# A four-layer graph network on one core: index loads over 96 partitions, counting on two engines, the step table before the first node table, and padding rows of their own

## The reference, cut to what matters

```
h = x @ W                                   # layer 0, attention (self loops included)
alpha = softmax over edges of dst of leaky_relu(h@att_src [src] + h@att_dst [dst])
x = layernorm(x + sum over edges of alpha * h[src] + bias)

f = ssp(edge_attr_128 @ We1 + be1) @ We2 + be2          # layer 1, filtered messages
x = layernorm(x + x + ssp(segment_sum((x @ Wn)[dst] * f, by src) @ W2 + b2) @ W3 + b3)

x = layernorm(x + normalised graph convolution(x @ W.T) + b)       # layer 2
x = layernorm(x + relu((x + segment_sum(x[src])) @ W1 + b1) @ W2 + b2)   # layer 3
```

## Time and profile before

| | us |
|---|---|
| median of 3 runs | 5233.95 (5231.75 to 5244.96) |
| profiled execution | 5240.87 |
| its span | 5239.2 |
| PE busy | 2666.3 (51%) |
| DVE busy | 2713.4 (52%) |
| ACT busy | 1384.4 (26%) |
| POOL busy | 3533.9 (67%) |

### The profile page before, as it was taken

The page is one execution under the profiler, slowest core; times in us unless marked ns, Lnnn a source line. Parts: engine busy times, 40 slices in busy tenths (PEclk is TensorE's granted clock), DMA queues, the critical chain, the costliest instruction groups (busy, mean ns, idle before and its releaser), DMA issues. The chain is left out here.

```text
span 5239.2 us, 54126 instructions
## 1 busy us (share of the span) xinstructions
PE 2666.3 (51%) x13249; PEld 2200.9 (42%) x13329; DVE 2713.4 (52%) x7266; ACT 1384.4 (26%) x4147; POOL 3533.9 (67%) x3833
## 2 busy tenths in 40 slices
PE   1477777777688854344434534344443243434444
PEld 1355656556466643333333433333333233333333
DVE  2599888887788853333333433333333433333333
ACT  4497666666566720000000400000000200000002
POOL 0677777777255567777777377777777477777773
PEclk8799899998677765555555755555555555555556
DMA  3677666677377742122112122222223322222224
GB/s 76 175 172 173 160 162 159 161 173 152 64 228 230 231 123 53 51 53 53 52 51 52 45 56 52 52 52 53 53 53 49 58 53 51 51 51 53 53 53 52
DMA packets 430928, 489.98 MB, mean 94 GB/s; under 512 B 86459, under 2 KB 333071, under 8 KB 430614
## 3 DMA queue, kind: packets, MB, share of 16 engines
q0 software_dynamic: 131904, 288.49, 23.4%
q1 hardware_dynamic: 295828, 197.27, 14.0%
q10 hardware_dynamic: 2882, 0.70, 0.1%
HBM read 359.63 MB, written 126.50 MB: 93 GB/s over the span
## 5 line engine op out<-in xcount | busy, mean ns | idle before, releaser
L1521 PE MATMUL bank<-arena 128*128 128x128 f32 x4992 | 1276.9, 438 | 1952.1 <-DVE arena L893 1639.4
L1595 POOL DMA_INDIRECT arena<-node_table,pick x1664 | 1599.2, 961 | 633.3 <-issue 506.4
L1521 PEld LDWEIGHTS bank<-arena 128*128 128x128 f32 x4992 | 1111.7, 328 | 2117.1 <-DVE arena L893 1799.0
L879 DVE TENSOR_TENSOR acc<-acc,bank 128x128 f32 x2496 | 720.9, 289 | 2075.2 <-PE bank L1521 1785.9
L1595 POOL DMA_INDIRECT arena<-gat_table,pick x832 | 863.8, 1038 | 306.6 <-issue 247.8
L1595 POOL DMA_INDIRECT arena<-message_table,pick x832 | 799.6, 961 | 255.8 <-issue 253.2
L1194 ACT COPY xt<-bank 128x512 f32<-128x512 f32 (+1 forms) x39 | 21.6, 554 | 2128.7 <-PE bank L1465 2128.7
L893 DVE TENSOR_TENSOR arena<-iota_free,local 128x512 f32<-128x512 f32 x624 | 427.9, 686 | 7.2 <-DMA node_table<-x_sb 4.0
L1510 PE MATMUL bank<-arena 128*128 x1664 | 324.9, 356 | 50.8 <-DVE arena L908 45.3
L1510 PEld LDWEIGHTS bank<-arena 128*128 128x128 f32 x1664 | 278.3, 254 | 115.8 <-issue 115.8
L765 DVE SCALAR_TENSOR_TENSOR acc<-acc,arena,bank 128x129 f32 x832 | 287.5, 345 | 52.8 <-issue 24.2
(11 more groups left out here) (218 smaller groups left out, 3383.8 us busy)
## 6 DMA issues: line engine op xcount, KB each, us to landing
message_table<-arena POOLq DMA_DIRECT2D x208, 256.0 KB, 3.5
filter_table<-arena SPq DMA_DIRECT2D x196, 256.0 KB, 3.6
arena<-filter_table SPq DMA_DIRECT2D x624, 64.0 KB, 2.5
xt<-edge_cols SPq DMA_DIRECT2D x131, 256.0 KB
arena<-local_rows SPq DMA_DIRECT2D x208, 128.0 KB
arena<-node_table,pick POOLq DMA_INDIRECT x1664
arena<-edge_cols SPq DMA_DIRECT2D x65, 256.0 KB, 3.1
arena<-gat_table,pick POOLq DMA_INDIRECT x832
```

The lines of the kernel that those rows point to most:

```text
L879: e.tensor_tensor(a, a, bank[6 + t % 2][:, s * P:(s + 1) * P], ALU.add).then_inc(sums, 1)
L1521: ins = e.matmul(bank[6 + n % 2][:, s * P:(s + 1) * P], hot[n % 2][:, s, :], gathered[:, slot(n, s), 0:D], start=True, stop=True)
L1595: e.indirect_dma_start(out=dst, out_offset=None, in_=table, in_offset=bass.IndirectOffsetOnAxis(ap=index, axis=0)).then_inc(done, 16)
```

## The change

- `dst`, `src` and `ahead` are each loaded in three pieces: 96 rows, the 97th, and the short 98th. `dst` is first, then `ahead`, then `src`; `src` counts on the semaphore of `ahead`.
- ACT, and no longer SP, issues the load of `x`, ahead of its counting. ACT counts the first 29 borders of the first list and needs `dst` alone for it; DVE counts the other 20, by a comparison with an accumulated sum, behind its keys and ahead of the weights.
- The making of the layer-0 table moves behind the branch, into the step table: after `start_e` is made (L468), before DVE waits for the blocks and windows. The keys are stored ahead of the table, and the table is stored in five parts.
- The layer-0 table and both node tables get 128 rows more. A padding slot of partition p in `pick[0]` now picks row `NB*P + p`. The rows hold zeros, and `-BIG` as the logit in layer 0. SP writes them into the node tables ahead of its other zeros.

```diff
+ACT_BELOW = 29
+PARTS = {4: (0, 12), 8: (12, 24), 12: (24, 36), 15: (36, 45), len(TRIOS): (45, NB + 1)}
-        gat_table = dram("gat_table", [NB * P, D + 2])
-        node_table = [dram(f"node_table{k}", [NB * P, D]) for k in range(2)]
+        gat_table = dram("gat_table", [(NB + 1) * P, D + 2])
+        node_table = [dram(f"node_table{k}", [(NB + 1) * P, D]) for k in range(2)]
+        count_junk = flip[0:LP, :].bitcast(BF16)[:, 0:SF]
...
             def step_table(i, lo_bits, rows_of_table):
-                        own(e.tensor_scalar(same[:, :], local[0][:, :], P - 0.5, float(NB * P - 1), ALU.is_gt, ALU.mult))
+                        own(e.tensor_scalar(same[:, :], local[0][:, :], P - 0.5, pad_row[:, 0:1], ALU.is_gt, ALU.mult))
...
         def vector(e):
+            own(e.tensor_scalar(pad_row[:, :], iota_part[:, :], float(NB * P), None, ALU.add))
-            e.wait_ge(ahead_loaded, 32)
-            e.wait_ge(index_loaded, 64)
+            e.wait_ge(index_loaded, 48)
+            e.wait_ge(ahead_loaded, 96)
...
             e.tensor_copy(descents[:, :], descents[:, :]).then_inc(keys_made, 1)
+            q = 0
+            for b in range(ACT_BELOW + 1, NB + 1):
+                if q:
+                    after(q)
+                q = own(e.tensor_scalar(count_junk, list_index["dst"][:, :], float(b * P), 0.0, ALU.is_ge, ALU.add,
+                                        accum_out=below[0][:, b:b + 1]))
+            after(q)
+            below_by_v = own(e.tensor_scalar(below[0][:, ACT_BELOW + 1:NB + 1], below[0][:, ACT_BELOW + 1:NB + 1],
+                                             2.0, -float(SF), ALU.mult, ALU.add))
...
-            own(e.memset(acc[:, NB, :], 0.0))
+            own(e.memset(acc[:, NB, 0:D + 1], 0.0))
+            own(e.memset(acc[:, NB, D + 1:D + 2], -BIG))
-            for n in range(len(TRIOS) + 1):
-                ...                                  # L568 to L578, moved
...
             e.wait_ge(list_sorted, 1)
-            run(step_table(0, SRC_BITS, NB * P))
+            table_of_steps = step_table(0, SRC_BITS, NB * P)
+            next(table_of_steps)
+            next(table_of_steps)
+            for n in range(len(TRIOS) + 1):
+                ...                                  # L568 to L578
+            run(table_of_steps)
...
         def scalar(e):
+            e.wait_ge(cleared, 3)
+            e.dma_start(x_sb[:, 0:NB - 1, :], A["x"][0:FULL, :].rearrange("(b p) d -> p b d", p=P)
+                        ).then_inc(x_loaded, 16)
+            e.dma_start(x_sb[0:LAST, NB - 1, :], A["x"][FULL:N, :]).then_inc(x_loaded, 16)
-            run(count_below(0, list_index["dst"]))
+            run(count_below(0, list_index["dst"], ACT_BELOW))
...
         def tensor(e):
             def step_table(i):
-                e.wait_ge(counted, NB * (i + 1))
+                e.wait_ge(counted, ACT_BELOW + NB * i)
+                if i == 0:
+                    e.wait_ge(vec, steps_of_v["below"])
...                                                  # L1335 and L1345 move behind next(table_of_steps)
         def sync(e):
+            MAIN = LP // 16 * 16
+            def row_in(tile, flat, done):
+                e.dma_start(tile[0:MAIN, :], flat[0:MAIN * SF].rearrange("(p f) -> p f", f=SF)).then_inc(done, 16)
+                e.dma_start(tile[MAIN:LP - 1, :], flat[MAIN * SF:(LP - 1) * SF].rearrange("(p f) -> p f", f=SF)
+                            ).then_inc(done, 16)
+                last = flat.shape[0] - (LP - 1) * SF
+                e.dma_start(tile[LP - 1:LP, 0:last], flat[(LP - 1) * SF:].rearrange("(p f) -> p f", p=1)
+                            ).then_inc(done, 16)
+            e.wait_ge(cleared, 1)
+            row_in(list_index["dst"][:, :].bitcast(I32), A["dst"], index_loaded)
             e.wait_ge(cleared, 4)
+            row_in(ahead.bitcast(I32), A["dst"][1:E], ahead_loaded)
+            row_in(list_index["src"][:, :].bitcast(I32), A["src"], ahead_loaded)
...                                                  # weights as before
-            e.wait_ge(table_put, len(TRIOS))
-            e.dma_start(gat_table.rearrange("(b p) d -> p b d", p=P), acc[:, 0:NB, :]).then_inc(gat_table_out, 16)
             e.wait_ge(list_sorted, 1)
             e.dma_start(sorted_keys[0].rearrange("(p f) -> p f", p=P), keys[0][:, :]).then_inc(list_out, 16)
+            for n in PARTS:
+                b0, b1 = PARTS[n]
+                e.wait_ge(table_put, n)
+                e.dma_start(gat_table[b0 * P:b1 * P, :].rearrange("(b p) d -> p b d", p=P), acc[:, b0:b1, :]
+                            ).then_inc(gat_table_out, 16)
             e.wait_ge(gat_ready, 1)
+            for k in range(2):
+                e.dma_start(node_table[k][NB * P:(NB + 1) * P, :], zero_row[:, :]).then_inc(start_in, 16)
```

More of the change, by code:

```diff
@@ L254, in build_program @@
         pad_col = part([P, 1])
+        pad_row = part([P, 1])
         gat_w, att_prod = gathered[:, 4, :], gathered[:, 5, 0:D]
@@ L543, in vector @@
             e.tensor_copy(descents[:, :], descents[:, :]).then_inc(keys_made, 1)
+            q = 0
[7 more added lines that the diff above has]
+                                             2.0, -float(SF), ALU.mult, ALU.add))
+            steps_of_v["below"] = below_by_v
             e.wait_ge(weights_loaded, WEIGHTS_IN)
@@ L1012, in scalar, with count_below @@
             own = Count(sem("scalar_own"))
-            def count_below(i, index):
-                e.wait_ge(index_loaded, 64)
+            def count_below(i, index, last):
+                e.wait_ge(index_loaded, 48)
+                if i:
+                    e.wait_ge(ahead_loaded, 96)
                 e.wait_ge(off_bias_made, 1)
                 e.wait_ge(below_cleared, i + 1)
-                for b in range(1, NB + 1):
-                    if i * NB + b > 1:
-                        e.wait_ge(counted, i * NB + b - 1)
+                for b in range(1, last + 1):
+                    if i * ACT_BELOW + b > 1:
+                        e.wait_ge(counted, i * ACT_BELOW + b - 1)
                     e.activation(sign_junk[:, :], index[:, :], ACT.Sign, bias=off_bias[0:LP, b:b + 1],
@@ L1160, in scalar @@
             e.wait_ge(gat_ready, 1)
-            background = [count_below(1, list_index["src"]), second_list()]
+            background = [count_below(1, list_index["src"], NB), second_list()]
             for t in range(TICKS + 13):
@@ L1328, in tensor @@
                      ).then_inc(descents_summed, 1)
[L1329 to L1347, removed]
             e.wait_ge(fold_made, 2)
@@ L1370, in tensor @@
                              ).then_inc(f_done, 1)
-            run(step_table(0))
+            table_of_steps = step_table(0)
+            next(table_of_steps)
+            e.wait_ge(x_loaded, 32)
+            for n in range(len(TRIOS) + 1):
+                if n < len(TRIOS):
+                    if n:
+                        e.wait_ge(table_kept, n)
+                    for k, b in enumerate(TRIOS[n]):
+                        ins = e.transpose(bank[5][:, k * P:(k + 1) * P], x_sb[:, b, :], ident[:, :])
+                    ins.then_inc(table_turned, 1)
+                if n:
+                    n1 = n - 1
+                    e.wait_ge(table_kept, n)
+                    if n1 == 0:
+                        e.wait_ge(gat_w_made, 1)
+                    if n1 > 1:
+                        e.wait_ge(table_put, n1 - 1)
+                    for k in range(len(TRIOS[n1])):
+                        ins = e.matmul(bank[6 + n1 % 2][:, k * (D + 2):(k + 1) * (D + 2)],
+                                       xt[n1 % 2][:, k * P:(k + 1) * P], gat_w[:, :], start=True, stop=True)
+                    ins.then_inc(table_done, 1)
+            run(table_of_steps)
             e.wait_ge(selfs_made, 1)
@@ L1677, in gpsimd @@
                 e.wait_ge(f_out[k], 16 * FTICKS // 2)
-            e.wait_ge(start_in, 48)
+            e.wait_ge(start_in, 80)
             e.wait_ge(summed, STEPS)
```

36 lines of the change are left out of this document (20 added, 16 removed).

## The result

| | kernel before | changed kernel |
|---|---|---|
| median (lowest to highest) | 5233.83 us (5226.29 to 5244.96), 5 runs | 5142.0 us (5133.69 to 5151.31), 5 runs |
| profiled execution, span | 5240.87, 5239.2 | 5133.69, 5131.8 |
| first gather of layer 0 | 151.32 | 98.38 |

The ratio is 0.9825, 95% interval 0.9807 to 0.9844: faster by 91.8 us in the medians, where 78.7 were forecast (5155), and by 107.2 between the two profiled executions. The changed kernel was profiled in its fastest run, so I take the size of the gain from the medians and the places from the profile.

The account below looks back on a forecast made before the run. One setup chain bounds the time to the first gather, then POOL paces the gathers, and data the padding tails. Gains of 49.7 - 1 + 30 = 78.7 us from 5233.95 give 5155, range 5132 to 5188.

Parts of the forecast that it names:

- Loads: Start of setup: with 96-row pieces at the rate of `x`, `ahead` and `src` have landed at 17 us.
- the two ends: Landing of `ahead` and `src`: 10.5 us if the queues share evenly with `x`, 19 to 20 if behind all of it.
- Keys and counts: DVE's setup chain: comparison to last key copy 6.4 us, then 20 counts at 1.3 each, 26.1 with the rescaling.
- Rival 2: Setup: counts on DVE are cheap, 0.78 us each; 9 us more gained, time 5146; chance 0.10.
- Branch: DVE's branch before L617: 8.6 us of issue time, unchanged because it skips the same code.
- ACT: Setup beside DVE: issuing `x` holds ACT 10.8 us, 29 counts end at 52, ready at 58, needed at 64.7.
- L617 to the first gather: Late setup: table, `start_e`, blocks, windows and picks take 40.5 us, against 41.3 before.
- First gather: End of setup: first gather of layer 0 at 101.6 us instead of 151.3, 49.7 us earlier.
- the 1 us that I charged: After the first gather: SP's two more DMAs delay the start of the pipeline by 1 us at most.
- Padding rows: Ends of layers 0, 2 and 3: different rows bring ticks from 6.61 to 5.0 us, 10 each, 30 in all.
- The sum: Whole kernel: setup 49.7, less 1, plus padding 30, makes 78.7 us gained.
- Rival 4: Gathers of layer 0: moved tables and scattered rows raise their mean by 0.1 us, costing 83 us; 5255 to 5285; chance 0.04.

Follow-up runs that it names:

- the experiment: Kernel before with the list loads split over 96 partitions and the table's store moved behind that of the keys; one run, 5831.2 us.
- the second group: Four follow-up kernels on chip 2 beside the kernel before (5876 us); its pair: `x` by SyncE with 33 borders, 0.9904, against one padding row, 0.9925.

## Why the prediction was right, point by point

- **Loads, forecast 17, measured 16.1.** The queues do share: with `x` behind them the same lists were in at 9.89, against 15.22 and 14.83 in the kernels beside, so `x` costs them about 5 us. My value lay between the two ends, nearer the far one, and so did the measurement. By the Trainium skill (DMA: Bandwidth & Descriptors, section "Issuing engines are not separate DMA queues") DMAs of two issuers interleave on the same engines, and this pair of kernels agrees.
- **Keys and counts, 6.4 and 26.1, measured 6.4 and 25.3** (16.10 to 22.49, 22.49 to 47.81 with the rescaling). A count is 1.219 + 0.083 with overlap, 1.263 from one to the next. Rival 2 fell: a count takes 1.22 where the plain comparison took 0.69. The doubled rate that the Trainium skill (VectorE: DVE Perf Modes, section "The perf-mode tier table (the rule you actually need)") gives tensor_scalar on fp32 does not hold here for one that accumulates.
- **Branch, 8.6, measured 3.3. The step that failed on VectorE**: "it skips the same code, so it stays". The stall was set by what the DMA engines carried, and the change had moved the table's store away from it (3.38 against 8.67 in the experiment). It made L620 5.3 us earlier than forecast; with the 1.6 of smaller terms it stood at 54.2, not 61.1.
- **ACT, ready at 58 with 7 to 9 us in hand. That failed too, and cost little.** Issuing `x` held it 14.4 us, not 10.8, so the counts ended at 55.7 and became the last wait, 2.2 us for VectorE at L447. With `x` on SyncE and more borders on ScalarE the offsets came 8 to 10 us earlier.
- **L617 to the first gather, 40.5, measured 44.2.** 1.3 of the 3.7 is ACT's count: VectorE waited 2.2 for PE here, and 0.9 in the kernel before. The rest is the table: I gave it "11 us until the gather needs it", and it came last, 2.4 us behind the time that `pick` (95.22, and 0.7 to the gather) would have allowed. The data went at 14 to 36 GB/s for 5 us, not 290. With the words of `step_start` later the parts landed in 6.2 and 9.5 us. That case also stores earlier, and the words' own packets are over before the slow stretch, so the words are the likely cause and not isolated. The Trainium skill (DMA: Bandwidth & Descriptors, section "Specifications") asks for transfers of at least 512 bytes for full rate, smaller ones being read and written back; 14.4 us for 3.5 KB agrees.
- **First gather, 101.6, measured 98.4**: the branch (+5.3) and small terms less the two waits. Setup 52.9 instead of 49.7; the 1 us that I charged behind it has no row of its own.
- **Padding rows, 30, measured 25.5 behind the ends of layers 0, 2 and 3** (5.3, 9.0, 11.2), and part of the 5.7 inside layer 0. The mechanism holds (1.61 us a gather by itself); layer 0 gave about half of its 10. "At 6.6 still in layer 1" was wrong at no cost to the sum: its ticks went at 5.0 in the mean before as well (4.3 to 5.7). The reading of the kernel behind it was wrong, since layer 1's padding slots pick their own slot numbers and not one row.
- **The count of padding slots** was misread too. 832 steps hold 106,496 slots, so 6,496 are padding, 6% of all: 3,200 in whole steps, and 3,296 more in the last steps of the 49 blocks, not "3,296 less 3,200". Those are 67 a block on average, by the 13 ns a read an estimate of 0.9 us, below POOL's 1.25 a gather. So leaving them out did no visible harm, though a few blocks with nearly whole steps of padding may hold a part of what layers 2 and 3 gained inside.
- **The sum.** Setup 52.9 and tails 25.5 make 78.4, the forecast 78.7 with other parts. That they agree so closely is luck: the branch and the smaller terms gave 8 more, and the table, ACT and the tails 8 less. The median gained 91.8; the 13 left lie within what layers 0 to 3 scatter inside, and I have no cause for them.
- **Rival 4** (dearer gathers) did not come: 1039 ns in the mean on layer 0, as before.
- **What stays open**: what the padding rows do in the three later groups. Alone they brought nothing (ratios 1.0008 and 0.9997). Beside the rest of the change they may bring some 11 us (60.6 us less than before with them, 49 without; ratios 0.9894 and 0.9921, whose intervals overlap, from different groups of runs), but in the second group the pair that has them on one side only differs by no more than its first gather. Why the gathers come in lumps there isn't settled either.

## What to carry to other kernels

Look at the DMA rate of every load by itself (97 rows went at 26 GB/s, and over 200 when the 97th went alone), and give placeholder indices different rows: many reads of one row are slow in the transfers themselves, 82% of the DMA engines' time for 41 GB/s where 53 GB/s otherwise take 20%. Price a branch and a store by what else is in flight at that moment, since both changed by a factor of two or more with nothing of their own changed but the moment. And when one chain shrinks by 50 us, work out again to the microsecond who is second; here the second counter and the table's store stood 2 to 3 us behind and took what they could.

## What the runs showed of the hardware that was not expected

- Branching over a long block costs VectorE 3.3 us with the DMA engines nearly idle and 8.7 with a 3.2 MB store just issued; the instruction packet in the stall comes 1.4 us after its start in the first case and 6.3 in the second.
- Issuing a DMA of `x` (3.1 MB) held ScalarE 14.4 us beside the lists, and SyncE 9.0 behind them.
- 128 reads of one row take 1.61 us where a plain layer's gathers come at 1.42, and 1.65 where they come at 1.25.
- The same program took 5234 us at first and 5840 to 5893 in the three later groups, likely for other chips. The setup was alike (first gathers of the changed kernel at 98 and 104); what differs is that gathers come in lumps there. The 25 us of tails show in the first pair, and no median shows them later. The setup's gain carried over; that at the end of the layers was not seen again.
